# Zero rows that fill the contraction of the score products, in a decoder layer with routed experts

## The reference, cut to what matters

```
scores = einsum('bqhd,bkhd->bhqk', q, k) + einsum('bqr,bkr->bqk', q_rope, k_rope)[:, None]
w = softmax(where(causal, -inf, scores / sqrt(HD + D_R)))
attn = einsum('bhqk,bkhd->bqhd', w, v) @ W_o
```

## Time and profile before

| | before |
|---|---|
| median of the runs | 1665.43 us |
| profiled execution | 1660.45 us |
| its span | 1658.8 us |
| TensorE matmuls busy | 1426.1 us (86%) |
| VectorE busy | 772.4 us (47%) |
| ScalarE busy | 624.7 us (38%) |
| GpSimd busy | 320.4 us (19%) |
| mean granted TensorE clock | 0.860 |

### The profile page before, as it was taken

How to read it: one execution, slowest core, us unless ns; L and a number is a source line. 1 busy time by engine, 2 the same in 40 slices (tenths; PEclk the granted TensorE clock), 3 DMA queues, 4 the chain that set the end, 5 groups by cost and what they waited for, 6 DMA issues and landing times.

```text
span 1658.8 us, 25877 instructions
## 1 busy us (share of the span) xinstructions
PE 1426.1 (86%) x7580; PEld 988.4 (60%) x7581; DVE 772.4 (47%) x1640; ACT 624.7 (38%) x1327; POOL 320.4 (19%) x423
## 2 busy tenths in 40 slices
PE   3799999787999987999998789998529999999980
PEld 2555556654556564555656455555318888888870
DVE  3364453674544377444437735434653333333325
ACT  2114456312545521344652135454333333333323
POOL 3001112104111301301130131111142222222224
PEclk9758999956989985688998569899659999999995
DMA  4752203821221382122138212216231111111119
GB/s 144 203 90 40 35 20 108 193 44 53 39 39 41 102 179 46 46 39 39 41 107 174 46 44 39 39 41 231 81 86 51 51 51 51 51 48 51 51 38 304
DMA packets 87844, 131.86 MB, mean 79 GB/s; under 512 B 14945, under 2 KB 46945, under 8 KB 87585
## 3 DMA queue, kind: packets, MB, share of 16 engines
q1 hardware_dynamic: 74064, 100.98, 26.1%
q0 software_dynamic: 7936, 24.20, 4.1%
q10 hardware_dynamic: 5744, 5.43, 1.0%
HBM read 70.34 MB, written 40.98 MB: 67 GB/s over the span
## 4 chain that ended last, share of the span: by engine, by line
PE 66%; DVE 9%; issue 7%; DMA 6%; POOL 6%; ACT 2%; SPq 2%; DVEq 0%; POOLq 0%; ACTq 0%
PE ps L1012 12%; PE ps L717 10%; PE ps L694 9%; PE ps L718 8%; PE ps L999 8%; PE ps L732 7%; POOL xs L478 4%; DMA kas<-scr_k 3%; PE ps L672 2%; PE ps L698 2%; PE ps L1020 2%; DMA scr_q<-stg 1%; PE ps L902 1%; PE ps L982 1%; PE ps L927 1%
## 5 line engine op out<-in xcount | busy, mean ns | idle before, releaser
L1065 ACT ACTIVATE pT<-ps 128x512 f32<-128x512 f32 (+3 forms) x768 | 344.9, 493 | 458.8 <-PE ps L718 457.9
L717 PE MATMUL ps<-qs,kas 97*128 97x512 f32 (+2 forms) x768 | 319.9, 425 | 1.6 <-ACT pT L1065 0.5
L1196 DVE TENSOR_REDUCE nmax<-ps 128x1 f32<-128x640 f32 (+3 forms) x256 | 259.2, 1024 | 119.4 <-PE ps L698 113.3
L694 PE MATMUL ps<-kas,qs 96*128 96x512 f32 (+2 forms) x768 | 266.3, 438 | 36.7 <-DVE nmax L1196 15.8
L718 PE MATMUL ps<-qs,kbs 96*128 96x512 f32 (+2 forms) x768 | 278.0, 370 | 0.0
L717 PEld LDWEIGHTS ps<-qs,kas 97*128 97x128 f32 x768 | 156.5, 204 | 144.6 <-ACT pT L1065 96.3
L441 POOL TENSOR_SCALAR_AFFINE_SELECT pT<-pT 128x512 f32<-128x512 f32 x128 | 81.2, 635 | 644.2 <-ACT pT L1065 643.9
L694 PEld LDWEIGHTS ps<-kas,qs 96*128 96x128 f32 x768 | 162.6, 235 | 70.4 <-DVE nmax L1196 22.0
L1193 DVE TENSOR_REDUCE nmax<-ps 128x2 f32<-128x256 f32 (+3 forms) x128 | 105.1, 825 | 194.8 <-PE ps L698 193.4
L732 PE MATMUL ps<-pT,vaug 128*17 128x512 f32 (+3 forms) x1536 | 170.0, 515 | 18.4 <-POOL pT L441 18.3
L718 PEld LDWEIGHTS ps<-qs,kbs 96*128 96x128 f32 x768 | 156.5, 204 | 5.8
(11 more groups left out here) (193 smaller groups left out, 1727.0 us busy)
## 6 DMA issues: line engine op xcount, KB each, us to landing
xb<-xs SPq DMA_DIRECT2D x72, 129.0 KB, 2.1
qs<-rs SPq DMA_DIRECT2D x32, 256.0 KB, 6.0
scr_q<-stg SPq DMA_DIRECT2D x16, 512.0 KB, 2.7
scr_k<-stg SPq DMA_DIRECT2D x16, 512.0 KB, 3.5
kas<-rs SPq DMA_DIRECT2D x32, 256.0 KB, 6.1
qs<-scr_q SPq DMA_DIRECT2D x64, 128.0 KB, 5.4
kas<-scr_k SPq DMA_DIRECT2D x64, 128.0 KB, 6.3
kbs<-scr_k SPq DMA_DIRECT2D x64, 128.0 KB, 4.1
```

The lines of the kernel that those rows point to most:

```text
L694: ins = pe.matmul(ps[:, slot + bank, 0:n_k], qs[0:KROWS, g % 2, h, i * P:(i + 1) * P], kas[0:KROWS, g % 2, h, k0:k0 + n_k], start=True, st ...
L717: pe.matmul(o, kas[:, g % 2, h, j * P:(j + 1) * P], qs[:, g % 2, h, w0:q1], start=True, stop=False)
L1065: act.activation(pT[:, u % 2, h, 0:q1 - q0], ps[:, s2_bank(n), q0 - w0:q1 - w0], ACT.Exp, scale=ATT_SCALE).then_inc(s_exp, 1)
L1196: dve.tensor_reduce(nmax[:, k:k + 1], ps[:, slot:slot + 2, :].rearrange("p s n -> p (s n)")[:, 0:(i + 1) * P], AX.X, ALU.max, negate=True) ...
```

## The change

The three operand tiles are allocated with all 128 partitions. `MROW = P - 1 = 127` is the new place of the row of ones and of the row of maxima. Partitions 96 to 126 of all three tiles are zeroed by GpSimd, and the products take partitions 0 to 126 (L694, L718) or 0 to 127 (L717). The results are the same, since the added terms are zero. The zeroing is done again wherever other data has lain over those partitions: in the set-up for `kbs`, set 0 of `qs` and set 1 of `kas`; once per batch for set 0 of `kas` (`zero_keys`) and for `kbs`; once, after the set-up's constants are read, for set 1 of `qs`. TensorE waits for these.

```diff
+MROW = P - 1
-        kas = at("kas", [KROWS + 1, 2, HG, T], F32R, kas_at)
+        kas = at("kas", [P, 2, HG, T], F32R, kas_at)
-        qs = at("qs", [KROWS + 1, 2, HG, T], F32R, qs_at)
+        qs = at("qs", [P, 2, HG, T], F32R, qs_at)
-        kbs = at("kbs", [KROWS, HG, T], F32R, kbs_at)
+        kbs = at("kbs", [P, HG, T], F32R, kbs_at)
...
                 pool.memset(nhalf[:, :], -0.5).then_inc(s_init, 1)
+                pool.wait_ge(s_init, 8)
+                pool.memset(kbs[KROWS:MROW, :, :].bitcast(F32), 0.0).then_inc(s_zl, 1)
+                pool.wait_ge(s_zl, 1)
+                pool.memset(qs[KROWS:MROW, 0, :, :].bitcast(F32), 0.0).then_inc(s_zero, 1)
+                pool.wait_ge(s_zero, 1)
+                pool.memset(kas[KROWS:MROW, 1, :, :].bitcast(F32), 0.0).then_inc(s_zero, 1)
+                pool.wait_ge(s_zero, 2)
...
+                def zero_keys(b):
+                    pool.wait_ge(s_pr, b * N_PROJ + QK[3] + 1)
+                    pool.sem_inc(s_seen, 1)
+                    pool.wait_ge(s_rs, b * 4 + 4)
+                    pool.sem_inc(s_seen, 1)
+                    pool.memset(kas[KROWS:MROW, 0, :, :].bitcast(F32), 0.0).then_inc(s_zk, 1)
+                    pool.wait_ge(s_zk, b + 1)
+                    pool.sem_inc(s_seen, 1)
                 for m in range(4):
                     rope_add(0, m)
                     rope_low(0, m)
+                zero_keys(0)
                 for s in s_stg:
                     pool.wait_ge(s, 64)
                 pool.dma_start(xa[:, :, :], x[1].rearrange("(t p) d -> p t d", p=P)).then_inc(s_x, 16)
+                pool.wait_ge(s_xm, 3)
+                pool.wait_ge(s_xm_read, B + 3)
+                pool.memset(qs[KROWS:MROW, 1, :, :].bitcast(F32), 0.0).then_inc(s_zero, 1)
+                pool.wait_ge(s_zero, 3)
...
+                    if then:
+                        pool.wait_ge(s_tri, (b + 1) * NG * len(DIAG))
+                        pool.sem_inc(s_seen, 1)
+                        zero_keys(b + 1)
                     power(0, 0, s_ve1, s_pow1)
                     power(0, 1, s_ve1, s_pow1)
...
                     power(1, 1, s_ve2, s_pow2)
+                    if then:
+                        pool.wait_ge(s_t7, (b + 1) * NT)
+                        pool.sem_inc(s_seen, 1)
+                        pool.wait_ge(s_pow2, (b + 1) * 2)
+                        pool.sem_inc(s_seen, 1)
+                        pool.memset(kbs[KROWS:MROW, :, :].bitcast(F32), 0.0).then_inc(s_zl, 1)
+                        pool.wait_ge(s_zl, b + 2)
+                        pool.sem_inc(s_seen, 1)
...
-                    sp.dma_start(kas[KROWS:KROWS + 1, p, :, :].bitcast(F32), one[0:HG * T // P, :]).then_inc(s_ones[p], 16)
+                    sp.dma_start(kas[MROW:P, p, :, :].bitcast(F32), one[0:HG * T // P, :]).then_inc(s_ones[p], 16)
...
-                        sp.dma_start(qs[KROWS:KROWS + 1, g % 2, :, :].bitcast(F32),
+                        sp.dma_start(qs[MROW:P, g % 2, :, :].bitcast(F32),
                                      nmaxT[:, :].bitcast(F32)).then_inc(s_mx, 16)
...
-                            ins = pe.matmul(ps[:, slot + bank, 0:n_k], qs[0:KROWS, g % 2, h, i * P:(i + 1) * P],
-                                            kas[0:KROWS, g % 2, h, k0:k0 + n_k], start=True, stop=not diag)
+                            ins = pe.matmul(ps[:, slot + bank, 0:n_k], qs[0:MROW, g % 2, h, i * P:(i + 1) * P],
+                                            kas[0:MROW, g % 2, h, k0:k0 + n_k], start=True, stop=not diag)
...
-                    pe.matmul(o, kbs[:, h, j * P:(j + 1) * P], qs[0:KROWS, g % 2, h, w0:q1],
+                    pe.matmul(o, kbs[0:MROW, h, j * P:(j + 1) * P], qs[0:MROW, g % 2, h, w0:q1],
                               start=False, stop=True).then_inc(s_s2, 1)
...
+                        pe.wait_ge(s_zk, b + 1)
+                        if isinstance(b, int) and b == 0:
+                            pe.wait_ge(s_zero, 1)
                         pe.wait_ge(s_vc, b * 4 + 4)
...
+                            pe.wait_ge(s_zl, b + 1)
                             heads_here(b, 1, 0)
...
+                pe.wait_ge(s_zero, 3)
                 with pe.Fori(0, B - 1) as b:
```

More of the change, by code:

```diff
@@ L222, in layer @@
         s_w, s_cx, s_c = sem("w_loaded"), sem("ctx_loaded"), sem("consts_loaded")
+        s_zero, s_zk, s_zl = sem("unused_rows_zeroed"), sem("unused_keys_zeroed"), sem("unused_klow_zeroed")
         s_wh, s_wl, s_init = sem("w_high_done"), sem("w_low_done"), sem("init_done")
```

## The result

The changed kernel took 1648.03 us (median of four runs, 1644.98 to 1651.51) against 1669.1 us of the kernel before on the same chip: ratio 0.9884, with a 95% interval of 0.984 to 0.9929. It is faster by 1.2%, clear of no change, but within 2% and at about half of the forecast's gain of 36.5 us. The ratio is that of the undisturbed runs, so a run of the kernel before that took 2596.22 us is left out of it. The profiled run took 1644.98 us against 1660.45 us, a difference of 15.5 us.

What follows compares the result with a forecast made beforehand. TensorE was taken to bound the kernel, below full clock because score products over 96 or 97 rows do not restore it; 25+7+2+1.5+1 = 36.5 us off 1660.45 gives 1624, median 1629, range 1612 to 1660.

Steps and rivals of the forecast that it cites:

- term 5: Zeroing memsets on GpSimd, in set-up and borders: 3.6 us each, all hidden behind waits, so 0 cost.
- Term 1: Head groups 1 and 2 of each batch: fewer and shorter clock falls, gain 25 us (20 to 28.8).
- Term 2: Restart after the scatters at a batch's start: shorter half-clock stretches on TensorE, gain 7 us (0 to 9).
- Term 3: First batch: group 0 gains 2 us, the score-only stretch before it 1.5 us (0 to 4).
- Term 4: Border between batches: clock expected to stay as it is, gain 1 us, ends -2 and +6.
- rival (b): Clock rises but falls again as work fills half the time: half the gain goes, median 1647; chance 0.12.
- (a): Zero rows do not count for TensorE's clock: nothing changes but hidden memsets, median 1665; chance 0.16.
- (c): Set-up: three memsets of 10.2 us each make everything after the first barrier 16.8 us later; chance 0.04.
- some 87 us behind the last exact score: Sign in the borders: the first scatter still stands this far behind the previous batch's last exact score.

Runs made afterwards that it cites:

- the second profile: Another profiled run of the unaltered changed kernel, on another chip; that repeat measured 1643.87 us, ratio 0.9888 to the kernel before.
- experiment 4: Changed kernel with each border memset (keys and low keys) cut into 16 pieces of 256 elements: 1627.88 us, ratio 0.9747 to the kernel before.
- experiment 1: Changed kernel with all zeroing kept but score products back over 96 and 97 rows, plus one SP wait: 1680.66 us, ratio 1.0088 to the kernel before.
- the copy's packets: Changed kernel with zero rows copied by DMA on SP's queue instead of memsets: keys alone 1713.06 us, keys and low keys 1718.51 us.
- experiments 4 and 5: Changed kernel with border memsets cut into 16 pieces: both 1627.88 us, then the key memset alone 1633.98 us, the low-key memset alone 1636.23 us.

## Why the prediction was wrong

**The failed step is term 5, zeroing at 0.** "Both are covered even at 10.2 us" was read from the waits in GpSimd's own queue. Those waits were there and stayed (13.50 and 32.69 before; in the border shown, 14.52 and 30.00). What the step did not ask is what else the instruction holds while it runs. The waits' own releasers are VectorE's (ve L1242, slots L1403), and it is VectorE that the memset stops. The holds, with what followed them, cost 18 to 20 us where the forecast had 0. The duration itself was well costed: 3.51 us measured, 3.6 forecast, in set-up and border alike; the set-up's barrier did not move (the mark of the earlier trace rows at 20.43 is now at 20.66).

**Term 1, groups 1 and 2**, 25 forecast, 22.2 measured. The reading of the earlier trace rows held: fewer falls (two, as forecast), each of 3.4 us. Over the 8 x 44.1 us of undisturbed groups 28.8 us stood before and 6.6 stand now, where I had left 3.4. The missing 3 us: groups without a fall took 44.2 to 44.7 us, against 43.8 to 44.3 before. The difference is within what profiles of one kernel differ by: the second one has no fall in these groups, 355.4 us, and so a gain of 26.2.

**Term 2, restart**, 7 forecast; group 0 of the three later batches fell by 157.7 - 151.8 = 5.9. What followed the scatters was at half clock for 9.6, 9.6 and 13.0 us in these groups, against 15.9, 22.8 and 26.9.

**Term 3, first batch**, 3.5 forecast, 4.2 + 3.0 = 7.2 measured. I had capped the stretch of maxima by VectorE's pace; time at half clock ahead of the first exact product fell from 53.7 to 33.2 us. The term was twice what I took, and just over its upper ends of 4 and 2.1. The cap of 2.1 took 44.1 us for an undisturbed group 0, but this one took 43.2 with 4.4 us at half clock in it. Of the 4.2 us, the second profile shows 0.1 (106.5 us up to the first exact product, 45.6 of them at half clock), so that part may be luck.

**Term 4, border**, 1 forecast; without holds (experiment 4) the two parts came to +1.4 and -2.6, which is a gain of 1.2. It was right once term 5 is taken out.

**The sum.** 22.2 + 5.9 + 7.2 = 35.3 us of gain, less 18.3 in the borders and 1.5 elsewhere: 15.5. The kernel that undoes the step, experiment 4, has a span 35.3 us shorter than the one before (1658.8 to 1623.5), where the forecast's sum was 36.5. The measured 1648.03 us lies 19 us above the forecast's 1629, inside the stated 1612 to 1660, but only by the room left for rival (b). The forecast's own range has a slip in it: its ends, 18 and 50 us, give 1615 to 1647 on the scale of the median, and the 1642 written there belongs to the profile's scale.

**The rivals.** (a) fell: zero-valued rows do raise the clock (six groups at 1.00; experiment 1). The Trainium skill's rule that counts only how busy TensorE is ("TensorE: Matmul & The Clock Gate", Part 1: The HAM clock gate) does not cover this: the old products filled 10.20 of 10.20 us at 0.50, the changed ones 3.16 of 3.40, and behind these the clock was 0.99. (b) named nearly the right number, 1647, for a wrong reason: the clock held in the groups. (c) fell with memsets of 3.51 us. No rival had a memset that costs another engine time.

**The signs named beforehand** did their work. The border was to stay at "some 87 us behind the last exact score"; it came to 90.2, 90.7 and 91.7 us (before, 87.4, 83.1 and 83.8), and this pointed to the fault.

**What stays open.** Whether the border needs zeroing at all was not tried. That the write of the keys waits for the copy's packets is read from the trace and not isolated by a run. That the clock falls to 0.50 for 10.2 us *because* TensorE has less to do behind the hold is my reading; experiments 4 and 5 show only that stretch and hold go together (3.4 to 6.8 us at half clock in that part with the keys in pieces). Nor is it known how much of the loss is the clock's: with the memsets alone (experiment 1) the part had 6.8, 6.8 and 10.2 us at half clock and was about as long.

## What to carry to other kernels

Work put "in an idle engine's wait" is free only if it takes nothing that the awaited engine needs: look up who ends that wait, and whether the added instruction can hold it up. If it must stand there, cut it into short instructions; sixteen pieces cost GpSimd 1.3 us more per memset here, and the kernel got 20 us back. And where products over fewer than 128 rows keep the clock low, padding them with zero rows is worth a try; here the exact product alone gave the largest part.

## What the runs showed of the hardware

Rows of zeros count for the granted clock as others do: scores over 96 and 97 rows stayed at 0.50 for 10.20 us in which TensorE was busy throughout, over 127 and 128 rows 3.4 us were followed by 0.99, and 112 rows, with the exact product still over 128, did as well in the groups (359.8 against 358.8 us).

A memset of 31 x 4096 floats on GpSimd took 3.51 us and made a VectorE tensor_scalar beside it last 3.55 us instead of 0.47; in pieces of 256 elements, 0.31 us each, 0.88 at most. Beside the same kind of memset a VectorE tensor_tensor on PSUM kept its 0.69 us, reductions of PSUM (L1234) their 0.43 and 0.69, and ScalarE's copy of PSUM (L1114) its 1.02.

With the rows the time also spreads less: ten runs without them (experiment 1) spanned 32 us, ten with them (low keys in pieces) 12 us, though on another chip; the kernel before ran from 1646.87 to 1677.8 us in 13 runs, the kernel of experiment 4 on the same chip from 1625.13 to 1629.05 in 4.
